# Routing one-hots in bfloat16 with the token index innermost, and a new place for the second last window's residual, in a Mamba and mixture-of-experts kernel

## The reference

```python
x = x + _L0_attn_ref(_layernorm(x), ...)   # RMS norm, causal conv of 4 taps, selective scan over 512 steps, gate, W_out
x = x + _L0_ffn_ref(_layernorm(x), ...)
...
gate = softmax(xr @ Wg)                     # 4096 tokens, E = 16 experts
idx = argmax(gate, axis=1)
loc = sum((cumsum(onehot, axis=0) - 1) * onehot, axis=1)
valid = loc < C                             # C = 256 places per expert
...
h = relu(einsum('ecm,emf->ecf', dispatched, w1))      # 128 -> 512
expert_out = einsum('ecf,efm->ecm', h, w2)            # 512 -> 128
combined = gathered * (gates_s * valid)[:, None]
```

## Time and profile before

| | us |
|---|---|
| median of 3 runs | 734.86 |
| lowest and highest run | 732.03 and 735.17 |
| profiled execution: span of the page (its own time is not given beside it) | 732.8 |
| busy: PE, DVE, ACT, POOL | 610.7, 579.2, 581.7, 591.9 |
| gathers and scatters, L365 and L373, 64 issues | 33.2 and 32.0 busy |

### The profile page before, as it was taken

One profiled execution on the slowest core, in us unless ns is written; L12 is line 12 of the kernel. 1 busy time (PEld: TensorE's weight loads), 2 busy tenths in 40 slices (PEclk: granted clock), 3 DMA queues, 4 the chain that ended last, 5 costly groups with the idle time before them and its releaser, 6 DMA issues.

```text
span 732.8 us, 12812 instructions
## 1 busy us (share of the span) xinstructions
PE 610.7 (83%) x3988; PEld 475.9 (65%) x3988; DVE 579.2 (79%) x918; ACT 581.7 (79%) x1218; POOL 591.9 (81%) x567
## 2 busy tenths in 40 slices
PE   6698989889979889998988999898878794289774
PEld 4346667757757667766766766776667783179764
DVE  5577799899889989998998999889898982843221
ACT  4899989999998999999999999999988731233330
POOL 4488889999998989999998999998798860177774
PEclk9889899999989999999999999999988887589998
DMA  5341423245145313614542271244215202147561
GB/s 159 117 157 36 146 80 117 62 143 162 61 145 144 127 63 100 202 61 133 156 127 63 85 210 64 105 139 133 64 66 175 66 18 73 47 129 207 167 182 48
DMA packets 61735, 83.17 MB, mean 114 GB/s; under 512 B 14998, under 2 KB 47544, under 8 KB 61672
## 3 DMA queue, kind: packets, MB, share of 16 engines
q1 hardware_dynamic: 57896, 76.07, 34.0%
q0 software_dynamic: 2560, 6.08, 3.0%
q10 hardware_dynamic: 1216, 0.27, 0.2%
HBM read 69.81 MB, written 12.80 MB: 113 GB/s over the span
## 4 chain that ended last, share of the span: by engine, by line
ACT 27%; PE 22%; issue 17%; POOL 15%; DVE 13%; DMA 4%; POOLq 0%; SPq 0%; DVEq 0%; ACTq 0%
ACT z L1098 9%; POOL h L855 8%; DVE h L1367 7%; PE ps L1725 7%; ACT ps L989 7%; POOL h L869 4%; PE ps L1617 4%; DMA z<-rows_d,gidx 3%; PE ps L588 2%; PE ps L601 2%; ACT L1059 2%; ACT dtb L1059 1%; ACT xx L1016 1%; PE ps L1699 1%; ACT L1098 1%
## 5 line engine op out<-in xcount | busy, mean ns | idle before, releaser
L1367 DVE TENSOR_TENSOR_SCAN h<-ps,h 128x902 f32<-128x902 f32 x204 | 320.4, 1610 | 33.5 <-ACT ps L989 23.6
L855 POOL TENSOR_TENSOR h<-u,scr 128x640 f32<-128x640 f32 x208 | 298.2, 1462 | 2.4
L1725 PEld LDWEIGHTS ps<-h,ident 128*128 128x128 f32 x1632 | 239.4, 199 | 24.2 <-issue 21.8
L1725 PE MATMUL ps<-h,ident 128*128 128x160 f32 x1632 | 243.9, 310 | 3.3 <-issue 3.3
L1098 ACT ACTIVATE z<-dtb,asc 128x240 f32<-128x240 f32 x576 | 237.4, 485 | 0.3
L989 ACT ACTIVATE ps<-z 128x820 f32<-128x820 f32 (+1 forms) x208 | 138.2, 689 | 16.0 <-DVE h L1367 8.9
L869 POOL TENSOR_TENSOR h<-h,scr 128x960 f32<-128x960 f32 (+1 forms) x52 | 106.0, 2038 | 1.1 <-DVE h L1383 1.1
L1418 DVE TENSOR_TENSOR h<-h,ps 128x640 f32<-128x640 f32 (+2 forms) x169 | 106.5, 642 | 0.2
L1617 PE MATMUL ps<-xnT,wT 128*128 128x488 f32 x144 | 77.2, 652 | 0.3 <-ACT xnT L974 0.3
L1699 PE MATMUL ps<-sqb,sel 128*8 128x32 f32 x832 | 33.6, 195 | 37.6 <-ACT sqb L999 27.7
L1699 PEld LDWEIGHTS ps<-sqb,sel 128*8 128x8 f32 x832 | 27.2, 91 | 53.0 <-ACT sqb L999 45.7
(11 more groups left out here) (193 smaller groups left out, 820.2 us busy)
## 6 DMA issues: line engine op xcount, KB each, us to landing
scr<-b_d SPq DMA_DIRECT2D x52, 640.0 KB, 4.6
scr<-c_d SPq DMA_DIRECT2D x52, 240.0 KB, 4.4
z<-in_L_ffn_w_dram SPq DMA_DIRECT2D x32, 256.0 KB, 3.1
cdg<-cdg_d SPq DMA_DIRECT2D x52, 93.8 KB, 2.1
xx_d<-xx SPq DMA_DIRECT2D x8, 256.0 KB, 2.0
xxr<-xx_d SPq DMA_DIRECT2D x8, 256.0 KB, 2.8
rows_d<-h2b SPq DMA_DIRECT2D x16, 120.0 KB, 2.0
rows_d<-xxr SPq DMA_DIRECT2D x16, 120.0 KB, 2.3
```

Source lines behind the costliest of these rows:

```text
L855: pool.tensor_tensor(o.rearrange("p (n b) t -> p n b t", b=B), us.unsqueeze(1).to_broadcast([P, nn, B, SEG]), bb[:, S % RING, n0 * BS:(n0 ...
L1367: dve.tensor_tensor_scan(hs, region(G)[:, 0:(r1 - r0) * SLOT], hs, 0.0, ALU.mult, ALU.add).then_inc(gscan, 1)
L1725: pe.matmul(ps[:, YB, 0:H * BS], ident[:], hr[:, :, n * B:(n + 1) * B, 0:SEG], start=(n == 0), stop=False)
```

## The change

It has two parts. In the routing, all one-hots and their factors become 16-bit and are laid out with the token index innermost; the comparison constants are expanded to full size ahead of the logits' load (`route_consts`, called between the two last copies of logits; `iofull` by ACT). The fine one-hot is made in two DVE operations of 16 tokens each instead of 24 and ACT's 9, and the places product moves from POOL to DVE. PE reads both operands of the slot and gate matmuls with a step of 32 elements of 2 bytes. The subtraction that Exp reads moves behind the copy of the totals. `cum` is written by expert innermost, and `loc` is a reduction over adjacent elements.

In the scan's end, `add_out(7)` and `out_stats(7)` move from segment 50 to segment 51 behind `last_y`; `out_pool(7)` moves behind the last product on POOL; PE projects window 8 before it transposes window 7. Two waits are added: DVE's `out_stats(o)` waits for the scale of the window before (`rstd2_done`), and POOL's power in `out_pool(o)` waits for the normalization of the window before (`h2_ready`).

```diff
-        LOCH, LOACT = 4, 8
+        LOP = 2
-        ohlo = ohlo.bitcast(BF16).rearrange("p (k c) -> p k c", c=P)
+        ohlo = ohlo.bitcast(BF16).rearrange("p (l k) -> p l k", k=NT)
+        iofull, o = take(z, o, NT * P // 2)
...
@@ pool_tail
-            pool.wait_ge(hi_ready, 1)
-            pool.tensor_tensor(idw[:, :, 1, :], ohhi, place.unsqueeze(2).to_broadcast([P, NT, NS]), ALU.mult).then_inc(places_in, 1)
@@ act_tail
+            act.wait_ge(iol_ready, 1)
+            act.copy(iofull, iol.unsqueeze(2).to_broadcast([P, P, NT])).then_inc(full_ready, 1)
...
-            for k in range(LOACT):
-                ins = act.activation(dist[:, k, :], iol, ACT.Square, ...)
-            act.activation(ohlo[:, NT - LOACT:NT, :], dist, ACT.Exp, scale=-200.0).then_inc(lo_act, 1)
@@ route_consts, before the last copy of logits
+            dve.tensor_scalar(iomk..., iol[:, 0:E].unsqueeze(1).to_broadcast([P, NT, E]), float(-E), None, ALU.add)
+            dve.tensor_scalar(iome..., iol[:, 0:E].unsqueeze(2).to_broadcast([P, E, NT]), float(-E), None, ALU.add)
+            step(dve.tensor_scalar(iot, iol[:, 0:NS].unsqueeze(2).to_broadcast([P, NS, NT]), float(-NS), None, ALU.add))
@@ dve_tail
             step(dve.tensor_reduce(mx, v3(lga), AX_X, ALU.max))
-            dve.tensor_tensor(v3(em), v3(lga), mx..., ALU.subtract).then_inc(em_ready, 1)
-            step(dve.scalar_tensor_tensor(out=v3(cand), in0=v3(em), scalar=0.0, in1=iom..., op0=ALU.is_equal, op1=ALU.mult))
-            step(dve.tensor_reduce(im, v3(cand), AX_X, ALU.min))
+            step(dve.tensor_tensor(v3(eq), v3(lga), mx..., ALU.is_equal))
+            step(dve.tensor_tensor(pick, eq, iomk, ALU.mult))
+            step(dve.tensor_reduce(im, v3(pick), AX_X, ALU.min))
+            step(dve.tensor_tensor(e3(ohe), e3(iome), im.unsqueeze(1).to_broadcast([P, E, NT]), ALU.is_equal))
...
             dve.tensor_copy(tot, e3(cum)[:, :, NT - 1]).then_inc(tot_ready, 1)
+            dve.tensor_tensor(v3(em), v3(lga), mx..., ALU.subtract).then_inc(em_ready, 1)
...
-            step(dve.tensor_tensor(cum, cand, ohe, ALU.mult))
-            step(dve.tensor_reduce(loc, cum.rearrange("p (e k) -> p k e", k=NT), AX_X, ALU.add))
+            step(dve.tensor_tensor(v3(cum).rearrange("p k e -> p e k"), e3(cand), e3(ohe), ALU.mult))
+            step(dve.tensor_reduce(loc, v3(cum), AX_X, ALU.add))
...
-            for k in range(NT - LOACT):
-                dve.tensor_scalar(ohlo[:, k, :], iolb, lo[:, k:k + 1], None, ALU.is_equal).then_inc(lo_ready, 1)
+            dve.tensor_tensor(ohhi, iot, tile_no.unsqueeze(1).to_broadcast([P, NS, NT]), ALU.is_equal).then_inc(hi_ready, 1)
+            dve.tensor_tensor(idw[:, 1], ohhi, place.unsqueeze(1).to_broadcast([P, NS, NT]), ALU.mult).then_inc(places_in, 1)
+            dve.wait_ge(full_ready, 1)
+            for q in range(LOP):
+                k0, k1 = q * NT // LOP, (q + 1) * NT // LOP
+                dve.tensor_tensor(ohlo[:, :, k0:k1], iofull[:, :, k0:k1], lo[:, k0:k1].unsqueeze(1).to_broadcast([P, P, k1 - k0]),
+                                  ALU.is_equal).then_inc(lo_ready, 1)
@@ pe_tail
-                ins = pe.matmul(ps[:, SLOTS, 0:2 * NS], ohlo[:, k, :], idw[:, k].rearrange("p f c -> p (f c)"),
+                ins = pe.matmul(ps[:, SLOTS, 0:2 * NS], ohlo[:, :, k], idw[:, :, :, k].rearrange("p f c -> p (f c)"),
-                    ins = pe.matmul(ps[:, GATES, 0:3 * NS], ohlo[:, k, :], gtw[:, k].rearrange("p f c -> p (f c)"),
+                    ins = pe.matmul(ps[:, GATES, 0:3 * NS], ohlo[:, :, k], gtw[:, :, :, k].rearrange("p f c -> p (f c)"),
@@ out_pool and ln_stats
+                at_least(pool, h2_ready, o)
+                at_least(dve, rstd2_done, read)
@@ POOL's program
-                if s == 3 and w == NWIN - 1:
-                    out_pool(o)
...
             c_last(NSEG - 1)
+            out_pool(NWIN - 2)
             out_pool(NWIN - 1)
@@ DVE's program
                     last_y()
+                    add_out(o)
+                    out_stats(o)
                     gate_y(S - 1)
...
-                elif s == 2 and out_:
+                elif s == 2 and out_ and w < NWIN - 1:
                     add_out(o)
-                    if w == NWIN - 1:
-                        out_stats(o)
...
             evac_lg(NWIN - 2)
+            route_consts(dve, steps_of_routing)
             evac_lg(NWIN - 1)
@@ PE's program, last segment
+                    project_out(NWIN - 1)
                     turn_h2(o)
-                    project_out(NWIN - 1)
                     route(o, S)
```

More of the change, by code:

```diff
@@ L287, in mamba_moe, with half @@
         cand, o = take(dAf, o, NT * E)
-        ohe, o = take(dAf, o, NT * E)
-        dist = dAf[:, 0:LOACT * P].rearrange("p (k c) -> p k c", c=P)
+        def half(o, n):
+            t, o = take(dAf, o, n // 2)
+            return t.bitcast(BF16), o
+        ohe, o = half(o, NT * E)
+        eq, o = half(o, NT * E)
+        pick, o = half(o, NT * E)
+        iomk, o = half(o, NT * E)
+        iome, o = half(o, NT * E)
         cum, o = take(dAf, o, NT * E)
@@ L292, in mamba_moe @@
         mx, o = take(dAf, o, NT)
-        im, o = take(dAf, o, NT)
+        im, o = half(o, NT)
         loc, o = take(dAf, o, NT)
         upper, o = take(dAf, o, NT)
-        tile_no, o = take(dAf, o, NT)
-        lo, o = take(dAf, o, NT)
+        tile_no, o = half(o, NT)
+        lo, o = half(o, NT)
         se, o = take(dAf, o, NT)
@@ L300, in mamba_moe @@
         part1, o = take(dAf, o, 1)
-        place, o = take(dAf, o, NT)
+        place, o = half(o, NT)
         held, o = take(dAf, o, NS)
@@ L305, in mamba_moe @@
         iol, o = take(dAf, o, P)
[L306 to L309, removed]
         empty, o = take(dAf, o, NS)
@@ L466, in dve_tail @@
-            step(dve.memset(e3(keep)[:, :, 0], 0.0))
+            dve.tensor_copy(iol, iota_i[:]).then_inc(iol_ready, 1)
+            dve.wait_ge(iol_ready, 1)
+            step(dve.memset(keep.rearrange("p (e k) -> p e k", k=NT)[:, :, 0], 0.0))
+            dve.tensor_scalar(iomk.rearrange("p (k e) -> p k e", e=E), iol[:, 0:E].unsqueeze(1).to_broadcast([P, NT, E]),
+                              float(-E), None, ALU.add)
+            dve.tensor_scalar(iome.rearrange("p (e k) -> p e k", k=NT), iol[:, 0:E].unsqueeze(2).to_broadcast([P, E, NT]),
+                              float(-E), None, ALU.add)
@@ L470, in dve_tail @@
-            dve.wait_ge(em_ready, 1)
-            step(dve.scalar_tensor_tensor(out=v3(cand), in0=v3(em), scalar=0.0, in1=iom.unsqueeze(1).to_broadcast([P, NT, E]),
-                                          op0=ALU.is_equal, op1=ALU.mult))
-            step(dve.tensor_reduce(im, v3(cand), AX_X, ALU.min))
-            step(dve.tensor_tensor(e3(ohe), iom.unsqueeze(2).to_broadcast([P, E, NT]),
-                                   im.unsqueeze(1).to_broadcast([P, E, NT]), ALU.is_equal))
+            step(dve.tensor_tensor(v3(eq), v3(lga), mx.unsqueeze(2).to_broadcast([P, NT, E]), ALU.is_equal))
@@ L1261, in _, with ln_stats @@
             dve.memset(cdg[:], 0.0).then_inc(const_dve, 1)
-            def ln_stats(v, src, b6, m2, ready, count, step, done):
+            def ln_stats(v, src, b6, m2, ready, count, step, done, read=0):
                 dve.wait_ge(ready, count)
```

51 lines of the change are left out of this document (24 added, 27 removed).

## The result

The changed kernel was **slower**, by 0.7%: median 738.95 us (735.21 to 740.9, 17 runs) against 732.62 for the kernel before (731.37 to 735.46, 17 runs), ratio 1.0069 with a 95% interval of 1.0054 to 1.0084. At 733 us that is 5.1 us (4.0 to 6.2); the two medians themselves lie 6.3 us apart. The forecast was 1.5 us less, so its sign was wrong. The profiled execution has a span of 739.1 us, 6.3 more than the one before.

The account below looks back on a forecast made before the run. POOL's issuing of transfers was taken to pace the expert stage, so an earlier `gidx` moves the end. Terms -1.5 - 0.5 - 1.4 + 1.9 = -1.5 us, carried onto the median 734.86, gave 733.4; range 729.3 to 739.0.

Parts of the forecast that it names:

- The first reading: Four engines about 80% busy until the last sixth, then none; there POOL's 64 indirect transfers, 1.31 us apart, set the pace.
- Part 1: Scan's end: the new residual order gains 0.9 us and a later clock fall 0.6; -1.5 us (-0.9 to -2.4).
- the restart's 0.95 us: Scan's end on DVE: with the 1.97 us residual and statistics moved away, the restart comes 0.95 us earlier.
- The 0.6 us for the clock: Last transposes and router matmuls: PE works longer, so the clock may fall later; 0 to 1.5 us gained, 0.6 taken.
- Rival (d): Scan's end: reordering gives nothing, as the second last window's logits come late and delay the last transposes; 734.9 us, chance 0.06.
- Part 2: Routing on DVE up to `lo`: 16-bit steps bring `pick` and `ohe` from 0.69 to 0.43 us; -0.5 us (0 to -0.5).
- Rival (c): DVE's 16-bit products run at one element at a time, as in L505; 736.4 us, chance 0.10.
- Part 3: One-hots and slot sums: coarse one-hot to `gidx` 6.83 us against 8.23, slot matmuls 0.118 us each; -1.4 us.
- Rival (a): Slot and gate matmuls: PE's strided reads cost nothing; 730.0 us, chance 0.28.
- Part 4: Gate matmuls, first expert: strided columns add 3.85 us, less 1.2 slack and 0.7 from an earlier clock rise; +1.9 us (0 to +2.6).
- The slack of 1.2 us: Expert stage: second output finished at 661.78, its scatter issued at 663.03, so 1.2 us of delay was taken as free.
- The point at which I let the total turn: Total as -10.1 + 80 c, c being the price of a 64-column matmul; it turns at c = 0.127 us.

Follow-up runs that it names:

- h_pairs: Changed kernel with one-hots token outermost, dense for PE, and each token's factor held twice side by side; ratio 0.9959 to the kernel before.
- e_order: The kernel before with the new residual order alone, its two added waits included; ratio 1.0002 to the kernel before.
- g_after: The changed kernel unedited, as a control on a chip with the long expert stage; ratio 1.0001 to the kernel before.
- g_lop4: Changed kernel with the fine one-hot in four operations of 8 tokens; ratio 1.0000 to the kernel before.
- f_gates_wdense: Changed kernel whose gate matmuls load dense weights but still read strided columns, summing wrong products; ratio 1.0003 to the kernel before.
- h_after: The changed kernel unedited, repeated on a chip with the short expert stage; ratio 1.0069 to the kernel before.
- h_gates_early: Changed kernel with its strided gate matmuls moved ahead of the first expert's transposes; ratio 1.0032 to the kernel before.

## Why the prediction was wrong

The first reading was a little loose: in slices 36 to 39 of the page before, PE stands at 8, 9, 7 and 7 tenths, so not every engine drops in the last sixth. That POOL's transfers set the pace there holds all the same (h_pairs above).

**Part 1 (-1.5 us): mostly not there.** In e_order and g_after the restart's 0.95 us came as worked out (12.63 and 12.65 us between the last two restarts, before 13.60), and the projection started 0.98 us sooner, where 0.88 was forecast. The term that failed is the projection's own length: "after the projection's end at 608.0" is 605.97 + 2.05, as long as before. I had taken the state sum at 6.26 us from a trace in which some 3.5 us of it ran at the half clock. It ran at the full clock in 4.58, so the gap was now PE's, 2.06 us, the clock fell behind it, and the projection took 2.75 us. That left 0.3 us. In the first trace of the changed kernel even the restart came no sooner (13.60 again): the state sum of segment 50 took 7.21 us, most of it at the half clock, in place of 6.26, and that is the same 0.95. The distance of the restarts is 12.6 in eleven of the fourteen traces with the new order, 13.6 in two and 11.0 in one. The 0.6 us for the clock did not come either: it fell during 613 to 614 as before, and the last transposes and router matmuls took 1.12 and 1.89 us. The whole part is worth 0 to 0.3 us. Rival (d) had it at nothing too, but for another reason, which did not occur: window 7's logits were copied at 614.45, ahead of the last transposes at 616.21.

**Part 2 (-0.5): right.** From the first reduction to the coarse one-hot 8.47 us in place of 9.00. The strided write took 1.02 (631.01) and the dense reduction at 632.07 took 0.69. Rival (c) is out: the 16-bit products took 0.42 us for 512 elements and 0.69 for 1024, which is 0.53 ns an element, half the 1.04 of before. No row of before had such operands, all 16-bit and with step 1.

**Part 3 (-1.4): right, a little short.** From the coarse one-hot to the `gidx` write 7.10 us in place of 8.23, so -1.1. The price of a slot matmul was 0.128 us, forecast 0.118, and g_lop4 shows that it sets the end. Rival (a), no cost at all, is out. The rule of the Trainium skill (SBUF — State Buffer, "Door 1: The DMA port swizzle"), that accesses with one element in each 16-byte line pay, holds for PE's moving columns: 1.76 ns each in f_gates_wdense. What the Trainium skill, TensorE: Matmul & The Clock Gate, says in "Weight-path perf modes", that 16-bit weights load in four chunks at once, packed or strided, agrees with 2.11 us for the 32 gate matmuls with strided weights, 0.5 more than with dense ones.

**Part 4 (+1.9): the step that turned the sign.** The gate matmuls' own time was forecast at 5.6 us and is 5.79. What failed is the clause behind it, "If the clock rises earlier, up to 1.5 comes back. I take 0.7". The clock did the opposite: it fell during the slow matmuls, and `down` and `up` behind them took 3.65 and 2.34 us instead of 2.02 and 1.89 in the trace of before, 2.1 more; the first `up` was no faster (3.64 against 3.25). Counted from the `gidx` write, the gate matmuls start 0.76 us later than before (11.20 against 10.44), they take 4.03 more until `down` starts, and from there to the end of the second output it is 2.03 more: 28.29 in place of 21.47. The slack of 1.2 us was wrong too. From an output's end to its scatter 0.8 us pass in the changed kernel (668.72 to 669.54), so of 663.03 - 661.78 only 0.4 was free. POOL's part of the delay is therefore 6.4 us, in two waits (4.81 for the first output, 2.02 for the second) where I had one of 2.6, and the stage is 6.2 us longer. The upper bound of the part, 2.6, was too low, since it held only the matmuls' own time. How much of it is the clock differs from trace to trace: in h_after `down` and `up` took only 1.1 us more than before, but the gate matmuls started 11.73 us behind `gidx`, and the stage was 98.4.

**The sum:** 0 - 0.5 - 1.1 + 6.2 = +4.6, against the measured 5.1 (4.0 to 6.2). With Part 4 as I had it the sum would be +0.3, with Part 1 as I had it +3.1: Part 4 alone turns the sign, and Part 1 alone takes the gain away. The two first traces differ by 6.3, but 1.8 of that stood before the changed stretch (the restart of segment 50 at 587.23 in place of 585.45). That the changed kernel's 738.95 lies inside my range of 729.3 to 739.0 is luck: I had built the range on 734.86, the median of 3 runs, while that of 17 is 732.62; 5.1 us on top of 734.86 is 740.0, outside it. The point at which I let the total turn, 0.127 us a slot matmul, was met at 0.128, close to the 0.118 I took. But by that formula 0.128 gives +0.1 us; the other 5 come from the clause on the clock, the slack and Part 1. Of the two signs that I had named for a failed forecast one came: `gidx` came 1.7 us sooner, counted from the load, and not 2.

## What to carry to other kernels

A layout that makes one engine fast is paid by every other reader of the tile: price the step on the reader's side, per element read (here 1.76 ns a column on PE), and also what runs behind it, since here the slow matmuls left the clock at 1.2 GHz for the next ones. Where DVE wants adjacent 16-bit elements and PE dense rows, hold a broadcast factor in pairs; here both got what they want. And a gap in a trace into which work is to be moved must be checked against the clock at which its neighbour ran.

## What the runs showed that was not expected

- PE's granted clock fell from 2.4 to 1.2 GHz in the midst of gate matmuls with strided columns, PE busy throughout (654 to 655 in the changed kernel; 653 to 654 in f_gates_wdense, 0.60; 642 to 643 in h_gates_early, 0.92), and not with dense columns in the same place.
- A two-operand 16-bit product whose operands are rows of two elements, one of them repeated, runs as fast as a dense one: 0.69 us for 1024 elements.
- DVE's fast two-operand products and a POOL product at the same time slow each other: 4.07 against 2.35 us, and 2.83 against 1.91, so that together they last about as long as one behind the other.
- The same kernel has an expert stage of 92.5 us on one sort of chip and 108 on another, where DVE, ACT and PE stand still for several us at a time without a releaser in the trace. The changed kernel's stage was 6 us longer on the one sort and 1.5 us longer on the other (g_after, 109.6 against 108.1).
